# Graph attention start-up: the destination table copied and gathered first, the key weights loaded later, the first turns ahead of the counts

## The reference

```python
q = (h @ Wq).reshape(n, H, DK); k = (h @ Wk)...; v = (h @ Wv)...
e = einsum('ehd,ehd->eh', k[src], q[dst]) / sqrt(DK)
m = segment_max(e, dst);  ex = exp(e - m[dst]);  z = segment_sum(ex, dst)
a = segment_sum(ex / z[dst] * v[src], dst)
x = layernorm(h + a @ Wo, ln1)
f = relu(x @ W1 + b1) @ W2 + b2
out = layernorm(h + layernorm(x + f, ln2))     # N = 10000, D = 512, 8 heads
```

## Time and profile before

| what | value |
|---|---|
| median of three runs | 683.04 us (682.5 to 686.41) |
| profiled execution, first to last instruction | 682.0 us |
| PE busy | 641.5 us (94%) |
| DVE busy | 578.0 us (85%) |
| ACT busy | 528.3 us (77%) |
| POOL busy | 401.7 us (59%) |

### The profile page before, as it was taken

The page is one execution under the profiler, slowest core; times in us unless marked ns, Lnnn a source line. Parts: engine busy times, 40 slices in busy tenths (PEclk is TensorE's granted clock), DMA queues, the critical chain, the costliest instruction groups (busy, mean ns, idle before and its releaser), DMA issues. The chain is left out here.

```text
span 682.0 us, 10864 instructions
## 1 busy us (share of the span) xinstructions
PE 641.5 (94%) x3520; PEld 483.8 (71%) x3520; DVE 578.0 (85%) x1391; ACT 528.3 (77%) x1140; POOL 401.7 (59%) x363
## 2 busy tenths in 40 slices
PE   5999999999999999999999999999999999999950
PEld 2778877777777777777777777777778778675520
DVE  7668769879898898898889889988989898899792
ACT  2525269877888987988798889878878999698881
POOL 7267244867675865756776574864547726735423
PEclk9999999999999999999999999999999999999995
DMA  7844154644643745674474456455554824536452
GB/s 227 220 101 133 44 123 106 173 122 142 148 121 131 159 121 148 167 157 92 146 177 117 113 161 137 105 168 123 127 128 155 184 62 135 139 77 138 131 113 91
DMA packets 37747, 91.44 MB, mean 134 GB/s; under 512 B 8346, under 2 KB 9642, under 8 KB 37690
## 3 DMA queue, kind: packets, MB, share of 16 engines
q0 software_dynamic: 31536, 82.74, 47.6%
q1 hardware_dynamic: 6154, 8.01, 4.3%
HBM read 71.20 MB, written 20.99 MB: 135 GB/s over the span
## 5 line engine op out<-in xcount | busy, mean ns | idle before, releaser
L558 ACT ACTIVATE squares<-rows,nmean 125x512 bf16<-125x512 f32 x200 | 142.3, 713 | 41.5 <-DVE nmean L902 19.8
L412 POOL DMA_INDIRECT x_rows<-in_x_dram,node_idx x40 | 48.2, 1205 | 56.8 <-DVE rows L917 47.3
L416 POOL DMA_INDIRECT out_dram<-rows,node_idx x40 | 46.4, 1160 | 56.4 <-ACT rows L618 47.0
L473 POOL DMA_DIRECT2D x_rows<-in_L_gnn_ln_b_dram x40 | 52.9, 1372 | 31.1 <-DVE rows L821 21.7
L898 DVE SCALAR_TENSOR_TENSOR rows<-pF,rows 125x512 f32<-125x512 f32 x78 | 50.6, 686 | 23.2 <-PE pF L1103 22.5
L963 PE MATMUL pP<-wo_hi,aT_hi 128*125 128x512 f32 x160 | 65.9, 412 | 0.3 <-DVE aT_lo L848 0.3
L963 PE MATMUL pP<-xTs_hi,wv_hi 128*128 128x500 f32 x160 | 65.8, 411 | 0.0
L963 PE MATMUL pP<-xTd_hi,wq_hi 128*128 128x500 f32 x160 | 65.4, 409 | 0.1
L963 PE MATMUL pP<-xTs_hi,wk_hi 128*128 128x500 f32 x160 | 63.5, 397 | 0.6 <-ACT q L539 0.6
L963 PE MATMUL pP<-wo_lo,aT_hi 128*125 128x512 f32 x160 | 63.1, 394 | 0.0
L963 PE MATMUL pP<-wo_hi,aT_lo 128*125 128x512 f32 x160 | 63.0, 394 | 0.0
(11 more groups left out here) (197 smaller groups left out, 1760.6 us busy)
## 6 DMA issues: line engine op xcount, KB each, us to landing
x_rows<-in_L_gnn_ln_b_dram POOLq DMA_DIRECT2D x40, 512.0 KB, 6.7
dst_row<-in_dst_dram SPq DMA_DIRECT2D x9, 250.5 KB
q<-in_L_gnn_Wq_dram SPq DMA_DIRECT2D x1, 1024.0 KB, 5.6
rows<-in_L_gnn_Wk_dram SPq DMA_DIRECT2D x1, 1024.0 KB, 7.8
rows<-in_L_gnn_Wv_dram SPq DMA_DIRECT2D x1, 1024.0 KB, 6.8
x_rows<-in_L_gnn_Wo_dram SPq DMA_DIRECT2D x8, 128.0 KB, 6.0
xd<-in_x_dram,dst_idx POOLq DMA_INDIRECT x40, 4.6
xs<-in_x_dram,src_idx POOLq DMA_INDIRECT x40, 3.8
```

What stands on the lines that cost most here:

```text
L412: pool.indirect_dma_start(rows, None, x, bass.IndirectOffsetOnAxis(ap=table[:, column:column + 1].bitcast(U32), axis=0), bounds_check=N - ...
L416: pool.indirect_dma_start(out, bass.IndirectOffsetOnAxis(ap=table[:, column:column + 1].bitcast(U32), axis=0), rows, None, bounds_check=N ...
L473: pool.dma_start(xr_wide[n], bass.AP(tensor=be2.tensor, offset=be2.offset, ap=[[0, P], [0, 2], [1, D]]), accum_op=ALU.add).then_inc(s[f"be ...
L558: ins = act.activation(squares[:, t, :], w[n][:, t, :], ACT.Square, bias=nmean[c][n][:, t:t + 1], accum_out=sq[c][n][:, t:t + 1])
```

## The change

Five things are moved, and two are split. No instruction on data is added or taken away.

- DVE copies dst_idx and the kept float copy dst_f within CAST, right behind the first transpose, and only then casts the source numbers and the next destinations. TABS keeps the other three.
- POOL makes the two number tables (a new step NUMBERS) behind the four gathers of xd instead of ahead of them.
- SP loads Wk behind the wait for xd_loaded, with Wv, instead of right behind Wq.
- On PE, TXD0 to TXD3 stand ahead of COUNT0 to COUNT2; on DVE, LQ and TXD0 to TXD3 stand ahead of CNT0 to CNT4. On ACT the list is the same as before.

```diff
-!COUNT3 -94502; !COUNT4 -90190; !ROFF -71911; !BITS -8816; TXD0 -189819 -22912 125030 125323 125345;
+!COUNT3 -94502; !COUNT4 -90190; !ROFF -71911; !BITS -8816; TXD0 -205000 -22912 125030 125323 125345;
...
             sp.dma_start(stage["q"], Wq.rearrange("(k p) n -> p k n", p=P)).then_inc(s["wq_loaded"], 16)
-            sp.dma_start(stage["k"], Wk.rearrange("(k p) n -> p k n", p=P)).then_inc(s["wk_loaded"], 16)
...
             on.wait_ge("xd_loaded", 64)
+            sp.dma_start(stage["k"], Wk.rearrange("(k p) n -> p k n", p=P)).then_inc(s["wk_loaded"], 16)
             sp.dma_start(stage["v"], Wv.rearrange("(k p) n -> p k n", p=P)).then_inc(s["wv_loaded"], 16)
...
-            pool.iota(iota_b, pattern=[[1, P], [0, T8]], base=0, channel_multiplier=0,
-                      allow_small_or_imprecise_dtypes=True).then_inc(s["iota_done"], 1)
-            pool.iota(column_b, pattern=[[1, NL]], base=0, channel_multiplier=0,
-                      allow_small_or_imprecise_dtypes=True).then_inc(s["iota_done"], 1)
...
-                if step == "GXD":
+                if step == "NUMBERS":
+                    pool.iota(iota_b, pattern=[[1, P], [0, T8]], base=0, channel_multiplier=0,
+                              allow_small_or_imprecise_dtypes=True).then_inc(s["iota_done"], 1)
+                    pool.iota(column_b, pattern=[[1, NL]], base=0, channel_multiplier=0,
+                              allow_small_or_imprecise_dtypes=True).then_inc(s["iota_done"], 1)
+                elif step == "GXD":
...
                     dve.tensor_copy(idx_f[0:CT, 1, :], idx_raw[0:CT, 1, :]).then_inc(s["idx_cast"], 1)
+                    on.wait_ge("tables_clear", 5)
+                    on.wait_ge("idx_turned", 1)
+                    dve.tensor_copy(dst_idx[0:R, :], pF[0][0:R, 0:CT]).then_inc(s["tables_done"], 1)
+                    dve.tensor_copy(dst_f, pF[0][0:R, 0:CT]).then_inc(s["dst_kept"], 1)
                     on.wait_ge("idx_loaded", 48)
...
-                    on.wait_ge("tables_clear", 5)
-                    on.wait_ge("idx_turned", 1)
+                    on.wait_ge("idx_turned", 2)
                     turned = pF[1][0:R, 0:3 * CT].rearrange("p (a t) -> p a t", a=3)
-                    dve.tensor_copy(dst_idx[0:R, :], pF[0][0:R, 0:CT]).then_inc(s["tables_done"], 1)
-                    on.wait_ge("idx_turned", 2)
                     dve.tensor_copy(src_idx[0:R, :], turned[:, 0, :]).then_inc(s["tables_done"], 1)
-                    dve.tensor_copy(dst_f, pF[0][0:R, 0:CT]).then_inc(s["dst_kept"], 1)
```

More of the change, by code:

```diff
@@ L26 @@
 !TURN -276034; !FOLD -51782; !OFFS -237181; !TURNF -205187; !COUNT0 -202748; !COUNT1 -198663; !COUNT2 -146723;
-!COUNT3 -94502; !COUNT4 -90190; !ROFF -71911; !BITS -8816; TXD0 -189819 -22912 125030 125323 125345;
+!COUNT3 -94502; !COUNT4 -90190; !ROFF -71911; !BITS -8816; TXD0 -205000 -22912 125030 125323 125345;
 TXS0 -102406 26305 131951 131437 131817; Q0 -138628 34546 131782 132194 129672; K0 -59911 65956 133983 133320 137209;
-V0 27356 105501 136738 136738 170605; O0 89451 141151 143013 157654 247834; TXD1 -186065 -14365 126120 126712 125690;
+V0 27356 105501 136738 136738 170605; O0 89451 141151 143013 157654 247834; TXD1 -204999 -14365 126120 126712 125690;
 TXS1 -100425 38188 132022 131705 131969; Q1 -106115 57936 132236 132221 132162; K1 -40813 69908 134313 133555 140512;
-V1 33080 113889 136894 136880 181017; O1 106767 141614 143149 165755 248144; TXD2 -166405 -7868 129028 130799 126518;
+V1 33080 113889 136894 136880 181017; O1 106767 141614 143149 165755 248144; TXD2 -204998 -7868 129028 130799 126518;
 TXS2 -88980 41299 132413 132381 134849; Q2 -86792 64359 132527 132551 134538; K2 -30166 75112 134486 134513 140777;
-V2 33666 129876 137553 138275 190162; O2 109181 144067 143559 170305 254002; TXD3 -155949 21677 129100 130978 126648;
+V2 33666 129876 137553 138275 190162; O2 109181 144067 143559 170305 254002; TXD3 -204997 21677 129100 130978 126648;
 TXS3 -83495 62551 132620 132450 134986; Q3 -70414 73944 132661 132967 137118; K3 -18228 75867 134696 134659 145042;
@@ L51 @@
 TXS0 -68603 20337 131158 130993 132478; Q0 -111138 42579 131621 131004 131070; V0 27197 127292 136963 137699 161962;
-TXD1 -146012 -9176 126544 127368 125657; TXS1 -67208 29303 131398 131008 132770; Q1 -73839 60821 132277 131401 133090;
-V1 37750 130738 138269 138390 173142; TXD2 -137214 -5075 128839 130614 126389; TXS2 -65419 35207 132157 131352 133268;
-Q2 -17185 62273 132574 132889 134345; V2 62190 138918 139637 142583 207890; TXD3 -118766 8616 128915 130664 126472;
+TXD1 -171195 -9176 126544 127368 125657; TXS1 -67208 29303 131398 131008 132770; Q1 -73839 60821 132277 131401 133090;
+V1 37750 130738 138269 138390 173142; TXD2 -171194 -5075 128839 130614 126389; TXS2 -65419 35207 132157 131352 133268;
+Q2 -17185 62273 132574 132889 134345; V2 62190 138918 139637 142583 207890; TXD3 -171193 8616 128915 130664 126472;
 TXS3 -48877 52021 132497 132466 133316; Q3 -10791 71890 132992 133126 134392; V3 74728 140001 140381 145994 218182;
@@ L77 @@
     "dve": """
-!CAST -263381; !FLAG -243336; !TABS -242836; !FILLI -241863; !FW -55094; !B1 -55229; !LQ -172721; !LK -85485;
+!CAST -263381; !FLAG -243336; !TABS -242836; !FILLI -241863; !FW -55094; !B1 -55229; !LQ -207000; !LK -85485;
 !LV -54432; !LO 76605; !CNT0 -198287; !CNT1 -179760; !CNT2 -159099; !CNT3 -97504; !CNT4 -91086; !RANK -79616;
-!DIG -211902; !LIST -79575; TXD0 -162172 -29587 125840 127315 124482; TXS0 -89151 40059 130890 130776 132032;
+!DIG -211902; !LIST -79575; TXD0 -206000 -29587 125840 127315 124482; TXS0 -89151 40059 130890 130776 132032;
 K0 -51732 66249 133633 132533 134452; W0 18249 122663 136307 136222 169476; N0 35421 125323 136834 136488 170118;
 G0 49521 129368 137409 137177 185919; L0 44048 128784 137153 137940 187035; H0 89910 140875 142983 151481 211814;
-TXD1 -161904 -24476 126177 127482 124895; TXS1 -88968 56437 131385 130810 132286;
+TXD1 -205999 -24476 126177 127482 124895; TXS1 -88968 56437 131385 130810 132286;
 K1 -49832 70573 134038 133868 136053; W1 29856 124303 136862 136864 179193; N1 42403 127213 136981 137078 182926;
 G1 68839 133170 137965 140178 189672; L1 64124 130892 138184 139311 192048; H1 97516 140880 143008 152925 213212;
-TXD2 -144446 7080 128832 130128 126147; TXS2 -67230 58549 131944 130850 132506; K2 -33982 77307 134316 133913 138039;
+TXD2 -205998 7080 128832 130128 126147; TXS2 -67230 58549 131944 130850 132506; K2 -33982 77307 134316 133913 138039;
 W2 61679 130905 137933 139380 191352; N2 70023 134152 138251 141899 191579; G2 76092 136480 140628 154187 213723;
-L2 72234 139296 139912 145223 200118; H2 101683 143459 143493 165349 227378; TXD3 -114588 26350 129097 130197 126490;
+L2 72234 139296 139912 145223 200118; H2 101683 143459 143493 165349 227378; TXD3 -205997 26350 129097 130197 126490;
 TXS3 -57609 63218 132044 131711 132622; K3 -31718 80817 134898 134139 143486; W3 68959 138928 138383 140291 192894;
@@ L119 @@
     "pool": """
-!SAVE -5825; !BIAS -40385; GXD -191598 -28838 122318 123741 124346; GXS -100305 39633 129311 131877 129664;
+!SAVE -5825; !BIAS -40385; !NUMBERS -191000; GXD -191598 -28838 122318 123741 124346; GXS -100305 39633 129311 131877 129664;
 FI 11329 78418 132148 139332 155267; GN0 71513 141862 142816 141861 224198; GE0 111452 138189 140544 141386 216328;
```

## The result

The changed kernel takes 685.63 us (median of 11 runs, 684.75 to 687.9) against 683.04 us (median of 11, 682.47 to 686.41). The ratio is 1.0037, with a 95% interval of 1.0023 to 1.0051: slower by 2.6 us, well within 1%. The forecast was 683.8 us with a range of 681.3 to 686.4. So the range holds the time, but it lies 1.8 us above the forecast, and at the price of the rival in which PE slows down, 685.4 us, to which the prediction gave a chance of 0.12. The prediction took 1% as about the least that can be told from no change; the interval here leaves no change out.

A forecast was written before the change was run, and what follows sets the result against it. The prediction took PE's list as the bound, so the start of Q0 sets the end: 683.0 us, +1.4 for Q0, -0.6 for the wait ahead of K, gives 683.8 us, with a range of 681.3 to 686.4.

The forecast's parts named there:

- the rival in which PE slows down: Gaps before Q0 drop PE to its slow rate at Q0: +1.6 us, 685.4 us in all; chance 0.12.
- fillers 0.41 apart behind COUNT2: Sign at PE's fillers just ahead of Q0: this spacing would show that PE had fallen to its slow rate.
- xd at 12.5, start of the gathers at 4.4: Start-up gathers: first starts at 4.4 instead of 7.68, xd is there at 12.5 instead of 15.81, bounds 12.0 to 14.5.
- The rival in which xd comes no earlier: Start-up gathers share DMA engines with other loads, so xd stays at 15.81: Q0 +4.7, 687.1 us; chance 0.04.
- the one of still sooner gathers: Fourth gather, with Wk out of the way, lands xd at 11.5: Q0 +0.4, 682.8 us; chance 0.18.
- The tables on DVE: DVE start-up: casts end about 4.0 instead of 5.03, LQ at 11.7; gain over 1 us, ending in a wait.
- Three tiles for 4.0 us behind the last lo part, and 1.27 to Q0: DVE writes CNT0 to CNT2 from 17.1 to 21.1; after COUNT2 and fillers Q0 starts at 22.4, 1.4 us later.
- From xd to the last lo part in 4.6 us: Turns and lo parts of xd: 5.07 us less about 0.45 for CNT2's tile, so lo parts end at 17.1.
- Wk, Wo and the wait ahead of K: Later Wk harmless, xs within 1 us of 24.95, and PE's wait before K's second part goes: -0.6 us.
- The hold-up of the gathers by DVE: About ten small DVE steps at 0.2 us hold POOL's gathers: xd 2 us late, 685.8 us; chance 0.08.
- The sum: Whole kernel: +1.4 us for Q0 and -0.6 for the wait ahead of K give +0.8, so 683.8 us.
- The forecast's late bound: Whole kernel, latest case of the forecast itself: Q0 3.4 us later, less 0.6, put at 685.9 us.

## Why the prediction was right, and where its sum was short

The range held the time, and the early xd, the bare tiles and the lost wait ahead of K came as the prediction had them. By its own sign, fillers 0.41 apart behind COUNT2, the case that it forecast is not the one that happened: the slow rival is, at a chance of 0.12. That the rival's 685.4 lies so near the measured 685.63 is in part luck, because its 1.6 us were worked out for Q0 and most of the loss arose earlier, at the turns.

**xd at 12.5, start of the gathers at 4.4.** Held: 12.88, and the first gather at 4.51. The prediction gave Wk a share in this without a number of its own; the runs show that it is needed for 2.2 of the 2.9 us, though alone it wins 0.1. The rival in which xd comes no earlier falls with it, and so does the one of still sooner gathers.

**The tables on DVE.** Held. The two casts take 0.34 together in place of 1.79, and LQ ends at 11.08 (forecast 11.7). In the earlier trace rows the pair of casts ended at 5.03, 0.14 behind the end of the number table that POOL wrote at the time. The Trainium skill, page "SBUF — State Buffer", section "SBUF: two separate sides", has it that VectorE, in its two-port modes, and GpSimd share a pair of ports which one instruction holds to its end while the other is blocked; the times of the trace agree, with one cast at 1.65 us and the other at 1.72 beside the table, and 0.21 and 0.24 without. This gain is real and ended in a wait, as forecast, though of 3.55 us in place of 2.1.

**Three tiles for 4.0 us behind the last lo part, and 1.27 to Q0.** The tiles held: 4.08 us from 19.44 to 23.52, and the order with Q0 ahead of the counts takes them off the path. The 1.27 was read off too long: in the kernel before, Q0 came 0.10 behind the last lo part and so 0.70 behind the start of COUNT2's fillers, where in the run with more fillers it comes 0.26 behind it. In that run CNT2 ends at 21.62 and Q0 follows 0.83 later; the 1.16 of the change is at the lower level. So the 22.45 of Q0 with more fillers meets the forecast's 22.4 because xd was 0.5 later and this stretch 0.4 shorter than forecast.

**From xd to the last lo part in 4.6 us.** This is the step that failed. It took 19.52 - 12.88 = 6.64, since both groups of turns ran at the lower level: 1.93 and 1.87 us in place of 1.07 and 1.23, and the fillers between them 1.92 in place of 1.03. In the run with more fillers the same steps took 4.60. The forecast placed the danger of PE's gaps only at Q0 and priced it there with 1.6 us. At the median the price was about right, 1.55, but most of it sits in the turns: in the profiled executions 2.04 us up to the last lo part, and only 0.47 in the first matmul of Q0. In these executions the whole is larger too: the span of 684.9 is 2.6 above the 682.3 of the run with more fillers. The profiled execution of the change took 686.61 us, 1.0 above the median of its runs. That the level can differ between executions is seen at the turns: up to there the run with Q0 ahead of the counts and 8 fillers has the same list on PE, and its first eight turns took 1.23 us in place of 1.93. How much of the scatter this makes is not shown.

**The decisive point of the slow rival.** Fillers at 0.41 apart behind COUNT2 were to show it. The two take 1.05 there in place of 0.60, which less 0.63 for the last one's own length is 0.42 apart. So it happened. The Trainium skill, page "TensorE: Matmul & The Clock Gate", Part 1, says that the clock falls to half in idleness and comes back under sustained work; the trace agrees in both levels and in what fillers do to them. In the changed kernel no filler and no turn of xd runs at the fast rate before the fillers behind TXD3: the eight fillers ahead of the wait took 3.60 us, 0.42 apart to the last. The chance of 0.12 was too low: the traces of before showed the eight fillers at 0.41 apart, and the changed order puts a wait of 2.5 us directly behind them, without the counts that kept PE at work in that wait.

**Wk, Wo and the wait ahead of K.** Held: the wait of 0.60 is gone, because PE comes there later. But xs is not within 1 us of 24.95, as forecast: SP's wait for it ended at 22.61, 2.3 sooner, so Wo was asked for that much sooner too. When Q0 was brought forward the wait was there again with 0.55.

**The hold-up of the gathers by DVE.** Small. The fourth gather started at 8.65, 0.06 behind the start of LQ, and took 1.50 us; in the run with Wk early it started 0.14 ahead of LQ and took 1.00. In the kernel before, the second gather of xs, started beside LQ, took 1.49 where the two behind it took 1.00 and 0.99. So half a microsecond is seen on one gather, not the rival's 2 us over ten small steps, and whether xd landed later by it is not shown.

**The sum.** The forecast's +0.8 us came out as +1.2 between the medians of the run with more fillers and of before, and as +0.3 between their profiled spans; the two differ because the profiled execution of before is itself above its median, by some 0.7 us. This is an estimate: nearly all timed runs are 1.7 to 1.8 us longer than their own spans, so that the span of 682.0 stands for about 683.7. The lower level adds 1.55 between the medians. The runs of the change scatter by 3.2 us, those with more fillers by 0.6. The forecast's late bound is 685.8 by its own sum, 683.0 + 2.8, and not 685.9.

## What to carry to other kernels

Work that lies in a wait costs nothing while the wait lasts longer, and when the wait is shortened the place of that work must be chosen anew: here the tiles of the counts moved from a wait to the stretch between the last input and the first product, and taking them behind that product took the loss of 2.6 us away; with more fillers besides it became a gain of 1.1. To have gathers land sooner, move the bulk loads queued ahead of them as well: here each of the two moves alone showed little of it, 0.8 and 0.1 of 2.9 us. When a start-up is rearranged, see that PE still has work in every wait up to its first product, since here the lower level cost at every short step in between and not only at the product.

## What was not expected of the hardware

PE's fall to the lower level did not always come with the gap. In the changed kernel it sat idle for 1.77 us ahead of COUNT0, ran COUNT0 and two fillers at the fast rate (0.69 and 0.60 us), and fell to the slow one at about 22.1, just ahead of COUNT1, with a gap of only 0.21 there; it rose again at about 25.5. In the run with Q0 ahead of the counts and 8 fillers the fall came while PE worked on the turns, which had started at 13.20: the granted clock is 1.00 from 12 to 14 us and 0.50 from 14 to 16, the first eight turns took 1.23, the fillers behind them 1.91 for four. In the run with Wk early, where PE had nothing to do from 10.4 to 15.04, it came within the gap, at about 13.9 (0.98 from 12 to 14, 0.50 behind).

The fp32 transposes follow this level as the products do: eight took 1.07 us at one and 1.93 at the other.

The granted clock reads 1.00 in every stretch up to 22 us in the changed kernel, although the turns and fillers from 12.88 to 18 run at the slow rate. Only from 22 on does the row say 0.52. In this trace, then, the length of the matmuls is the better witness that early.
